# A decoder block on one core: the second weight folding is ordered later, zeroing and expert-weight loads go one piece a unit, and the whole order is planned anew

## The chip, the cores and the metric

The kernel runs on one core of one Trainium2 chip. The metric is the device time of the program in microseconds, lower is better. Durations of single steps come from one profiled execution.

## The reference

For x of 8 batches x 112 tokens x 256 the block adds three sub-layers, each on a normalised x:

```python
x = x + self_attention(layernorm(x))                      # 16 heads of 16, causal, with biases
x = x + cross_attention(layernorm(x), ctx, ctx, mask)     # ctx: 8 x 375 x 256, per-head 16x16 Wq, Wk, Wv
x = x + moe_gated_slot_attention(layernorm(x))            # below
```

Cross attention projects with small 16x16 matrices and ends in `out @ Wo.T + bo`. The third sub-layer (2 of 8 experts per token) is:

```python
x = rms_norm(h, norm_w); scores = softmax(x @ Wg.T); top 2 experts of each token
# tokens sorted by (batch, expert); per expert k, v, f = x @ W[e].T ; q = x @ Wq.T
# a gated recurrence over chunks of 64 tokens, scattered back and weighted:
out = (restored * rw).sum(2); return rms_norm(out, gnorm_w) @ Wo.T
```

## The kernel before

**Stages and units.** All work is cut into named stages, each on one engine: T (TensorE), V (VectorE), A (ScalarE), P (GpSimd), S (SyncE, which issues most DMAs). Attention runs in 48 units: `("s", b, h)` is half of a batch's self-attention heads, `("c", b, g)` a quarter of its cross-attention heads. A unit is a first score product `S`, a row maximum `max` on V, a transpose `mT`, a subtraction `q2` on V, the scores again transposed `st`, an exponential `exp` on A, the product with the values `pv`, and a copy `oT`. `UNITS` lists them: index 0 to 5 are the self-attention of batches 0 to 2, then three cross units, two self units of batch b + 3 and a fourth cross unit for each batch.

**The order.** A class `Plan` simulates the five engines with the costs of `COST`, the lags of `LAG`, the landing times of `LANDS`, a rank for each stage shifted by `BIAS`, an earliest time `at`, and a `SLACK` per engine by which stages that could start at nearly the same time are compared by rank. It writes one list of stages per engine, and each engine's program is that list, in order, with waits on semaphores. A change of any cost or bias can reorder all five lists and the choice of PSUM banks.

**Combining weights.** `combine 0` multiplies the cross Wq and Wk into `bdq`. `combine 1` multiplies Wv and Wo into `fo`: four matmuls on T behind `wait_ge(l_wo, 32)`, a semaphore of two DMAs (`wvo` and a row of `rw_sb`), and a copy `fo` on V (line 1235). Its product is first used by the output projection of cross attention of batch 0, `oproj 1 0`. In the plan it has `at=19.5`, and `oproj 0` (self attention) needs it too, though the program of `oproj 0` waits for nothing of it.

**The experts.** Tokens are routed in two groups (batches 0 to 4, 5 to 7). Their rows are scattered by GpSimd into a DRAM buffer `xs_d` that must hold zeros first: eight writes of 896 KB from SyncE (stage `zero`, line 753), each behind the first score product of a unit of `Z_UNITS`: units 3, 5, 7, 9, 11 for the first group, 30, 32, 34 for the second. Expert weights come by one load of 256 KB and eight of 768 KB (stage `later`, lines 758 and 760) behind units 12, 14, ..., 28 (`L_UNITS`). GpSimd then scales them with the norm weight (stage `fold`, two instructions for each expert, line 1709), in two halves that each wait for their four loads. Then 29 tiles of 128 gathered rows are multiplied with their expert's weights (`pkf`, `pvx`), whose offset in `wm` TensorE reads from a register; a stage `regs` loads all registers of a group (16, then 13) from SBUF at once. The tiles' results go to DRAM, are gathered by token and scanned (`scan`).

**The start.** SyncE's first DMA is x of batches 0 and 1 together; the norm of batch 0 waits for it.

Of the kernel before, what the change touches and what calls it, by code (L numbers as in the profile page):

```python
# [4 lines left out]
NB, S, D, NK = 8, 112, 256, 375  # L5
KC, NC3 = 125, 3
NE = 8
GROUPS = ((0, 1, 2, 3, 4), (5, 6, 7))
# [5 lines left out]
GNT = [(2 * c + NE * 127) // 128 for c in GCAP]  # L14
GT0 = [sum(GNT[:g]) for g in range(NG)]
GBASE = [NE * sum(GCAP[:g]) for g in range(NG)]
NT = sum(GNT)
ZROW = NE * S * NB
TG = [g for g in range(NG) for _ in range(GNT[g])]
# [18 lines left out]
            + ([("s", b + 3, 0), ("s", b + 3, 1)] if b + 3 < NB else []) + [("c", b, 3)]])  # L38
Z_UNITS = [UNITS[3 + 2 * i] for i in range(len(GROUPS[0]))] + [UNITS[30 + 2 * i] for i in range(NB - len(GROUPS[0]))]
L_UNITS = [UNITS[12 + 2 * i] for i in range(1 + NE)]  # L40

# [5 lines left out]
        "kTx": (0.19, 0.36), "kp": (1.77, 1.95), "logits": (0.9, 1.06), "mTc": (0.15, 0.31),  # L47
# [3 lines left out]
        "pvc": (0.62, 0.78), "pvs": (0.43, 0.59), "pvx": (0.86, 1.03), "qTx": (0.76, 0.92),  # L51
        "qgT": (0.19, 0.36), "qk": (1.79, 1.95), "regs": (0.5, 0.5), "siT": (0.19, 0.36),
        "stc": (1.43, 1.59), "sts": (0.98, 1.14), "stx": (0.89, 1.07), "tm": (0.48, 0.65),
# [35 lines left out]
BIAS = {  # L89
    "T": {"G": -67, "Sc": -161, "Ss": -925, "cb": 292, "fT": 212, "fo": 935, "inf": -17, "kTx": -152,  # L90
          "logits": -273, "onT0": -97, "oproj0": -37, "oproj1": 169, "pkf": 342, "pvs": 1037, "pvx": 181,
# [8 lines left out]
}  # L100
SLACK = {"T": 0.3, "V": 0.1, "A": 0, "P": 0.15, "S": 0}

# [23 lines left out]
class Plan:  # L126

    LAG = {"AP": 0.14, "AT": 0.145, "AV": 0.035, "PV": 0.04, "TA": 0.1, "TP": 0.27, "TV": 0.107, "VA": 0.035, "VP": 0.09,
           "VT": 0.146, "VV": 0.0, "PA": 0.1, "PT": 0.15}
    LANDS = {"later": 8.0, "zero": 8.0, "gx": 2.6, "gk": 2.8, "scatter": 3.0, "kd": 2.5, "ldmask": 4.0, "ldctx": 3.0, "ldctxT": 4.0}  # L130
    UNIT = ("S", "max", "mT", "q2", "st", "exp", "pv", "oT")
# [33 lines left out]
    def build(self):  # L165
# [9 lines left out]
        add("V", ("combine", 0), 0.6, -230, [("T", ("combine", 0))])  # L175
        add("T", ("combine", 1), 0.9, -230, release=("V", ("combine", 1)), at=19.5)
        add("V", ("combine", 1), 0.75, -230, [("T", ("combine", 1))])
# [3 lines left out]
        for b in range(NB):  # L181
# [7 lines left out]
            for h in range(2):  # L189
# [8 lines left out]
            add("P", ("pad", b), 0.83, 100 * b - 120, [("A", ("ones", RT)), ("T", ("pv", ("c", b - 2, 3)))] + ld("ldctx", 2),  # L198
                at=18.0 if b == 0 else 25.0)
            add("P", ("mkb", b), 1.55, 100 * b - 110, [("P", ("mkT", b - 1)), ("V", ("max", ("c", b - 2, 3), 3))]  # L200
                + ld("ldmask", 2), at=15.0 if b == 0 else 23.0)
            add("P", ("mkT", b), 1.37, 100 * b - 110, [("P", ("mkb", b)), ("T", ("st", ("c", b - 2, 3)))])
# [61 lines left out]
    def output(self, k, b, r):  # L264
        add = self.add
        last = [("A", ("oT", ("s", b, h))) for h in range(2)] if k == 0 else [("A", ("oT", ("c", b, g))) for g in range(4)]
        add("T", ("nrm", k, b), 0.42, r, last + [("T", ("onT", k, b - 1))], ("V", ("nrm", k, b)))
        add("V", ("nrm", k, b), 0.78, r, [("T", ("nrm", k, b))])
        add("T", ("onT", k, b), 0.2, r, [("V", ("nrm", k, b)), ("T", ("oproj", k, b - 1))], ("A", ("onT", k, b)))
        add("A", ("onT", k, b), 0.36, 0, [("T", ("onT", k, b))])  # L270
        add("T", ("oproj", k, b), 0.9, r, [("A", ("onT", k, b)), ("V", ("combine", 1))], ("V", ("oproj", k, b)), at=17.0)
        add("V", ("oproj", k, b), 0.43, r, [("T", ("oproj", k, b)), ("P", ("xn", k, b)), ("P", ("xn", 1, b - 2 if k == 0 else b))])
# [200 lines left out]
def decoder_kernel(nc, x, ctx, ctxT, mask, maskT, watt, bself, wx, wxvo, rows, wrouter, wmoe, wo_moe,  # L473
# [5 lines left out]
    with root:  # L479
# [216 lines left out]
        def _(e):  # L696
# [19 lines left out]

            e.dma_start(xbo[:, 0:2, :], x[:, 0:2, :]).then_inc(l_x0, 16)
            e.dma_start(cst[:, 0:128], consts[:, 0:128]).then_inc(l_id, 16)
            e.dma_start(wqk[:, 0, :, :], watt[:, 0, :, :]).then_inc(l_wq, 16)
            e.dma_start(bqk[:, :], bself[:, 0:8]).then_inc(l_bqk, 16)  # L720
            e.dma_start(wqk[:, 1, :, :], watt[:, 1, :, :]).then_inc(l_wk, 16)
            e.dma_start(cst[:, C_CB:C_CB + 224], consts[:, C_CB:C_CB + 224]).then_inc(l_cm, 16)
            e.dma_start(wv[:, :, :], watt[:, 2, :, :]).then_inc(l_wv, 16)
# [53 lines left out]
        def _(e):  # L777
# [8 lines left out]
            for stage in order["T"]:  # L786
# [162 lines left out]
                elif what == "regs":  # L949
                    e.wait_ge(v_tab, N_TAB_INC * (b + 1))  # L950
                    e.load(regs[GT0[b]:GT0[b] + GNT[b]], eti[0:1, GT0[b]:GT0[b] + GNT[b]])
                else:
# [6 lines left out]
                    elif what == "pkf":  # L959
# [3 lines left out]
                        for i in range(2):  # L963
                            off = e.snap(regs[t], min_val=0, max_val=(NE - 1) * WC)
                            last = mm(ps[:, bk, 0:512], xsT[:, r, 128 * i:128 * i + 128], wm[:, bass.ds(off + i * 768, 512)],
                                      i == 0, i == 1)
                        last.then_inc(t_pkf, 1)
                    elif what == "pvx":
                        for i in range(2):
# [113 lines left out]
        def _(e):  # L1083
# [88 lines left out]
            for stage in order["V"]:  # L1172
                what, b, bk = stage[0], stage[-1], slot.get(stage, [None])[0]
                k = stage[1] if len(stage) == 3 else None
                if what == "stats":
                    v = st[:, b, k, :]
                    src = x1[:, b % 2, :] if k == 1 else xbo[:, b, :]
                    if k == 0 and b in (0, 2, 4):
                        e.wait_ge((l_x0, l_x, l_late)[min(b // 2, 2)], (16, 16, 48)[min(b // 2, 2)])
                    elif k == 1:  # L1180
                        e.wait_ge(v_x1, b + 1)
                    elif k == 2:
                        e.wait_ge(v_x2, b + 1)
# [12 lines left out]
                elif what == "consts":  # L1196
                    e.wait_ge(l_id, 16)
                    e.tensor_copy(idb[:, :], ident).then_inc(v_cst, 1)
                    e.wait_ge(l_cm, 16)
                    e.tensor_copy(cmb[:, :, :], cst[0:S, C_CB:C_CB + S].unsqueeze(1).to_broadcast([S, 2, S])  # L1200
# [682 lines left out]
```

## Time and profile before

| | |
|---|---|
| median of 3 runs | 462.94 us (459.88 to 474.88) |
| profiled execution, its own time | 463.49 us |
| its span, first to last instruction | 461.7 us |
| TensorE busy in the span | 432.3 us (94%) |
| mean granted TensorE clock | 0.985 |
| VectorE, ScalarE, GpSimd busy | 66%, 53%, 39% |
| DMA | 51.07 MB, mean 111 GB/s |

The span is 1.8 us shorter than the profiled execution's own time. A clock of 1.00 is the upper of TensorE's two levels (2.4 GHz), 0.50 the lower (1.2 GHz); a value between is a stretch that had both. Busy times of PE are modelled at their ends, so a stall inside the array doesn't show as idle time.

### The profile page before, as it was taken

The numbers are of one execution on the slowest core, as the hardware profiler recorded it, in microseconds if no ns is written. First come the engines' busy times: TensorE is split into PE (matmuls) and PEld (weight loads), VectorE is DVE, ScalarE is ACT, GpSimd is POOL, SyncE is SP. The second block draws the span as 40 slices with busy tenths as digits, with TensorE's granted clock in tenths as the row PEclk, the third lists the DMA queues.
The fourth block names the chain that finished last, engine by engine and source line by source line (L and its number), as shares of the span: only waits on it lengthen the run. The fifth ranks groups of instructions, "written<-read, shape, count | busy, mean of one in ns | idle before, by whom it ended". The sixth has DMA issues, their size and how long they took to land.

```text
span 461.7 us, 12854 instructions
## 1 busy us (share of the span) xinstructions
PE 432.3 (94%) x4632; PEld 317.0 (69%) x4632; DVE 306.3 (66%) x1034; ACT 244.8 (53%) x663; POOL 179.7 (39%) x240
## 2 busy tenths in 40 slices
PE   8879899999999899997979999899899999999997
PEld 6656576867667577664646666565578766988885
DVE  4736757487577577676786559995366675876663
ACT  5123233425443434443536778787675876777652
POOL 5451033132732752145332268626543214444320
PEclk9989979999999899999999999999999999999999
DMA  7848323544436335011210244445723332121202
GB/s 205 170 128 289 122 81 115 158 139 111 135 136 156 123 106 155 3 35 41 55 38 25 92 143 134 152 161 176 227 62 103 105 110 104 65 75 53 66 11 61
DMA packets 23918, 51.07 MB, mean 111 GB/s; under 512 B 3105, under 2 KB 13546, under 8 KB 23858
## 3 DMA queue, kind: packets, MB, share of 16 engines
q1 hardware_dynamic: 20018, 38.02, 26.5%
q0 software_dynamic: 3440, 11.15, 8.9%
q10 hardware_dynamic: 400, 1.10, 0.8%
q8 instruction: 39, 0.64, 0.6%
q14 instruction: 21, 0.17, 0.1%
HBM read 28.75 MB, written 21.50 MB: 109 GB/s over the span
## 4 chain that ended last, share of the span: by engine, by line
PE 76%; DMA 7%; DVE 5%; ACT 3%; issue 3%; another core or an unknown queue 3%; SPq 2%; ACTq 1%; POOL 0%; DVEq 0%; POOLq 0%
PE ps L781 67%; PE ps L784 9%; DMA rw_sb<-in_rows 3%; DMA kv<-kd_d,idk 3%; DVE jnk L1259 1%; ACT pT L1529 1%; DMA kd_d<-kd 1%; ACT u L1586 0%; ACT u L1584 0%; SPq L714 0%; DVE kd L1390 0%; DVE kd L1384 0%; ACT u L1588 0%; ACTq L1498 0%
## 5 line engine op out<-in xcount | busy, mean ns | idle before, releaser
L1529 ACT ACTIVATE pT<-ps 125x672 f32<-125x672 f32 (+1 forms) x96 | 60.6, 666 | 93.0 <-PE ps L781 84.1
L781 PE MATMUL ps<-wm,xsT 128*128 x232 | 83.4, 492 | 0.5 <-ACT xsT L1579 0.5
L1259 DVE CUSTOM_DVE_ANT_0 jnk<-ps,mkb 112x375 bf16<-112x375 f32 x128 | 63.6, 544 | 21.7 <-PE ps L781 21.7
L781 PEld LDWEIGHTS ps<-wm,xsT 128*128 128x128 f32 x232 | 41.0, 190 | 24.3 <-issue 21.6
L1758 POOL DMA_INDIRECT xs<-xs_d,idg x29 | 28.9, 997 | 29.8 <-PE ps L784 22.1
L781 PE MATMUL ps<-cxT,cqT 32*112 32x375 f32 x256 | 28.7, 518 | 7.3 <-ACT pT L1529 3.1
L781 PE MATMUL ps<-q,cxT 32*125 32x112 f32 x768 | 30.7, 291 | 0.0
L781 PEld LDWEIGHTS ps<-q,cxT 32*125 32x125 f32 x768 | 24.9, 190 | 7.8 <-issue 7.6
L1803 POOL TENSOR_TENSOR qg<-okb,dc 112x256 f32<-112x256 f32 x16 | 11.8, 736 | 42.4 <-ACT okb L1627 42.3
L1264 DVE TENSOR_REDUCE mxz<-ps 112x2 f32<-112x224 f32 x64 | 21.0, 383 | 10.3 <-PE ps L781 10.3
L1384 DVE SCALAR_TENSOR_TENSOR kd<-ps,u 128x512 f32<-128x512 f32 x29 | 19.9, 685 | 9.0 <-ACT u L1588 7.4
L781 PE MATMUL ps<-pT,cxp 125*32 125x112 f32 x768 | 25.7, 267 | 0.0
L1627 ACT ACTIVATE okb<-okb,sm 112x64 f32<-112x64 f32 x64 | 21.4, 338 | 8.1 <-DVE sm L1436 8.1
L781 PE MATMUL ps<-mkT,idb 125*125 125x336 bf16 x128 | 24.6, 315 | 0.9 <-DVE xbo L1284 0.6
L1584 ACT ACTIVATE u<-ps 128x512 f32<-128x512 f32 x29 | 17.3, 596 | 14.4 <-PE ps L781 13.7
L1741 POOL DMA_INDIRECT xs_d<-y,idu x16 | 15.8, 990 | 21.2 <-DVE idu L1347 18.0
L1687 POOL TENSOR_SCALAR st<-st 112x1 f32<-112x1 f32 x16 | 3.8, 235 | 49.2 <-DVE st L1186 49.2
L781 PEld LDWEIGHTS ps<-pT,cxp 125*32 125x32 f32 x768 | 17.8, 111 | 7.3 <-ACT pT L1529 2.7
L781 PEld LDWEIGHTS ps<-mkT,idb 125*125 125x125 bf16 x128 | 16.0, 139 | 8.4 <-issue 3.1
L1796 POOL DMA_INDIRECT kv<-kd_d,idk x16 | 15.3, 955 | 15.8 <-issue 6.9
L1722 POOL TENSOR_SCALAR mkb<-mki 112x375 bf16<-112x375 int32 x8 | 12.2, 1524 | 20.2 <-DVE mxz L1259 14.1
L781 PEld LDWEIGHTS ps<-cxT,cqT 32*112 32x112 f32 x256 | 9.8, 173 | 14.9 <-ACT pT L1529 7.7
(242 smaller groups left out, 1059.2 us busy)
## 6 DMA issues: line engine op xcount, KB each, us to landing
kd_d<-kd SPq DMA_DIRECT2D x29, 384.0 KB
xs_d<-xs SPq DMA_DIRECT2D x8, 896.0 KB, 4.2
wm<-in_wmoe SPq DMA_DIRECT2D x8, 768.0 KB, 4.3
cxT<-in_ctxT SPq DMA_DIRECT2D x32, 93.8 KB, 3.4
cx<-in_ctx SPq DMA_DIRECT2D x8, 375.0 KB
mki<-in_mask SPq DMA_DIRECT2D x8, 164.1 KB
mti<-in_maskT SPq DMA_DIRECT2D x8, 164.1 KB
out<-xbo SPq DMA_DIRECT2D x8, 112.0 KB, 1.8
```

Source lines behind the costliest of these rows:

```text
L781: return e.matmul(o, l, r, start=start, stop=stop)
L784: return e.transpose(o, i, ident[0:n, 0:n])
L1259: e.tensor_tensor_reduce(jnk[:, j % 2, :], ps[0:S, bk, 0:NK], mkb[:, b % 2, :], 1.0, -3e38, ALU.add, ALU.max, mxz[:, n % 2, 0, c:c + 1]).t ...
L1264: e.tensor_reduce(mxz[:, n % 2, :, :].rearrange("p i m -> p (i m)")[:, c:c + 113:112], ps[0:S, bk, 0:2 * S].rearrange("p (g n) -> p g n", ...
L1384: e.scalar_tensor_tensor(kd[:, t % RD, 0:512], ps[:, slot["pkf", t][0], 0:512], 0.0, u[:, r, :], ALU.min, ALU.subtract).then_inc(v_ls, 1)
L1529: e.activation(pT[0:w, n % RP, 2 * i:2 * i + 2, 0:m], ps[0:w, b0:b1 + 1:b1 - b0, 0:m], ACT.Exp).then_inc(a_pT, 1)
L1584: e.activation(u[:, r, :], ps[:, slot["pkf", t][0], 0:512], ACT.Abs).then_inc(a_sp, 1)
L1627: last = e.activation(w, w, ACT.Exp, bias=s4[:, h:h + 1], accum_out=s4[:, 4 + h:5 + h])
L1722: e.tensor_scalar(mkb[:, b % 2, :], mki[:, b % 2, :], 0.0, -1e20, ALU.is_equal, ALU.mult).then_inc(p_mkb, 1)
L1741: e.indirect_dma_start(out=xs_d.ap(), out_offset=bass.IndirectOffsetOnAxis(ap=idu[:, k, b:b + 1], axis=0), in_=y[:, b % RY, :], in_offset= ...
L1758: e.indirect_dma_start(out=xs[:, t % RX, :], out_offset=None, in_=xs_d.ap(), in_offset=bass.IndirectOffsetOnAxis(ap=idg[:, t:t + 1], axis= ...
L1796: e.indirect_dma_start(out=kv[:, t % RK, :], out_offset=None, in_=kd_d[g].ap(), in_offset=bass.IndirectOffsetOnAxis(ap=idk[:, b, j:j + 1], ...
```

## The change

- `combine 1` goes from rank -230, `at=19.5` to rank -40, `at=42.0`, and only `oproj 1` needs it in the plan. Its instructions and waits are the same.
- The eight zero writes stand behind units 14 to 21, the nine loads of `wom` and the experts' weights behind units 24 to 32.
- `regs` loads two registers of a group; the register of tile t + 2 is loaded on TensorE after the first product of tile t.
- x of batch 0 is loaded alone as the first DMA, x of batch 1 five DMAs later with a semaphore shared with the causal masks (one more DMA on SyncE's queue).
- Earliest times of `pad` and `mkb` of the first batches, some costs, nearly all biases, the slacks of V, A and P, and the planned landing of `gk` change, so the order of all engines is planned anew.

```diff
-Z_UNITS = [UNITS[3 + 2 * i] for i in range(len(GROUPS[0]))] + [UNITS[30 + 2 * i] for i in range(NB - len(GROUPS[0]))]
-L_UNITS = [UNITS[12 + 2 * i] for i in range(1 + NE)]
+Z_UNITS = [UNITS[14 + i] for i in range(NB)]
+L_UNITS = [UNITS[24 + i] for i in range(1 + NE)]
...
-SLACK = {"T": 0.3, "V": 0.1, "A": 0, "P": 0.15, "S": 0}
+SLACK = {"T": 0.3, "V": 0.2, "A": 0.15, "P": 0.2, "S": 0}
...
-        add("T", ("combine", 1), 0.9, -230, release=("V", ("combine", 1)), at=19.5)
+        add("T", ("combine", 1), 0.9, -40, release=("V", ("combine", 1)), at=42.0)
...
-                at=18.0 if b == 0 else 25.0)
+                at=26.0 if b == 0 else 30.0)
...
-                + ld("ldmask", 2), at=15.0 if b == 0 else 23.0)
+                + ld("ldmask", 2), at=19.0 if b == 0 else 29.0)
...
-        add("T", ("oproj", k, b), 0.9, r, [("A", ("onT", k, b)), ("V", ("combine", 1))], ("V", ("oproj", k, b)), at=17.0)
+        add("T", ("oproj", k, b), 0.9, r, [("A", ("onT", k, b))] + ([("V", ("combine", 1))] if k else []), ("V", ("oproj", k, b)), at=17.0)
...
-            e.dma_start(xbo[:, 0:2, :], x[:, 0:2, :]).then_inc(l_x0, 16)
+            e.dma_start(xbo[:, 0:1, :], x[:, 0:1, :]).then_inc(l_x0, 16)
...
+            e.dma_start(xbo[:, 1:2, :], x[:, 1:2, :]).then_inc(l_cm, 16)
...
-                    e.load(regs[GT0[b]:GT0[b] + GNT[b]], eti[0:1, GT0[b]:GT0[b] + GNT[b]])
+                    e.load(regs[GT0[b]:GT0[b] + 2], eti[0:1, GT0[b]:GT0[b] + 2])
...
+                        if t + 2 < NT and TG[t + 2] == TG[t]:
+                            e.load(regs[t + 2:t + 3], eti[0:1, t + 2:t + 3])
```

## Rows read from the trace of the kernel before

**Rows 1.** The page: span and the engines' busy time.

```profile
span 461.7 us, 12854 instructions
...
PE 432.3 (94%) x4632; PEld 317.0 (69%) x4632; DVE 306.3 (66%) x1034; ACT 244.8 (53%) x663; POOL 179.7 (39%) x240
```

**Rows 2.** Windows: length, busy time of PE, PEld, DVE, ACT, POOL, clock, DMA.

```profile
22.60:25.30 2.70, 0.00 (x0) 0.00 (x0) 0.00 (x0) 0.18 (x1) 1.52 (x2) 1.00 0.64 173
...
167.00:197.00 30.00, 29.68 (x453) 22.26 (x452) 20.72 (x76) 13.14 (x31) 6.31 (x9) 1.00 0.34 100
...
206.00:240.00 34.00, 27.30 (x419) 18.48 (x421) 25.07 (x112) 13.90 (x33) 14.44 (x18) 1.00 0.16 43
```

**Rows 3.** Waits of PE: in total, times, longest, in us.

```profile
PE ps L781 <- DMA rw_sb<-in_rows: 3.3, 1, 3.3
```

**Rows 4.** Timeline about the second folding: start, duration, engine, instruction.

```profile
22.18 0.39 DVE L1243 TENSOR_TENSOR q<-qkT,ps 128x224 f32<-128x224 f32 x1 [0.99 <-PE ps L784]
...
25.36 1.10 PE L781 MATMUL ps<-wvo 128*128 128x256 f32 x4 [3.29 <-DMA rw_sb<-in_rows]
...
26.50 0.69 DVE L1235 COPY fo<-ps 128x512 f32<-128x512 f32 x1 [3.93 <-PE ps L781]
```

**Rows 5.** Windows of TensorE alone: busy time, granted clock, DMA share.

```profile
25.00:28.00 3.00, 2.64 (x32) 0.82 0.33 111
28.00:31.00 3.00, 3.00 (x28) 0.61 0.32 121
49.00:55.00 6.00, 5.18 (x63) 1.00 0.53 178
55.00:58.00 3.00, 1.44 (x21) 0.94 0.00 0
58.00:61.00 3.00, 2.93 (x26) 0.50 0.82 279
```

**Rows 6.** Timeline about the register loads of both groups.

```profile
233.64 0.90 PE L781 MATMUL ps<-cxT,cqT 32*112 32x375 f32 x8 [0.41 <-issue]
...
290.83 0.16 DVE L1137 TENSOR_SCALAR eti<-etr 1x13 int32<-1x13 f32 x1
...
292.32 0.99 PE L781 MATMUL ps<-W,yq 112*128 112x224 f32 x4 [1.53 <-issue]
293.15 2.75 PE L781 MATMUL ps<-wm,xsT 128*128 x8
```

**Rows 7.** SyncE's queue: zero writes, weight loads, a batch's context load.

```profile
41.06 28.07 SPq L753 DMA_DIRECT2D xs_d<-xs  x4
...
79.32 0.35 SPq L760 DMA_DIRECT2D wm<-in_wmoe  x1
83.24 1.72 SPq L714 DMA_DIRECT2D cxT<-in_ctxT  x4
...
92.98 15.01 SPq L760 DMA_DIRECT2D wm<-in_wmoe  x3
...
157.40 8.99 SPq L753 DMA_DIRECT2D xs_d<-xs  x2
```

**Rows 8.** Timeline: folds, a norm beside one, first scatter, first gather.

```profile
115.36 7.09 POOL L1709 TENSOR_SCALAR wm<-wm,nwc 128x768 f32<-128x768 f32 x8
...
147.14 1.20 POOL L1741 DMA_INDIRECT xs_d<-y,idu  x1 [3.56 <-DVE idu L1347]
...
164.68 1.83 POOL L1709 TENSOR_SCALAR wm<-wm,nwc 128x768 f32<-128x768 f32 x2
...
165.01 0.73 DVE L1193 TENSOR_SCALAR xn<-x,st 112x256 f32<-112x256 f32 x1
...
232.31 1.03 POOL L1758 DMA_INDIRECT xs<-xs_d,idg  x1 [3.13 <-DVE eti L1137]
```

**Rows 9.** The chain that ended last, two of its pieces.

```profile
206.39 3.58 another core or an unknown queue
...
211.71 3.46 another core or an unknown queue
```

More of the change, by code:

```diff
@@ L47 @@
         "kTx": (0.19, 0.36), "kp": (1.77, 1.95), "logits": (0.9, 1.06), "mTc": (0.15, 0.31),
[1 row of a table removed]
[1 row of a table added]
         "okx1": (1.19, 1.35), "onT0": (0.19, 0.35), "onT1": (0.2, 0.38), "oproj0": (0.87, 1.03),
[1 row of a table removed]
-        "pvc": (0.62, 0.78), "pvs": (0.43, 0.59), "pvx": (0.86, 1.03), "qTx": (0.76, 0.92),
-        "qgT": (0.19, 0.36), "qk": (1.79, 1.95), "regs": (0.5, 0.5), "siT": (0.19, 0.36),
-        "stc": (1.43, 1.59), "sts": (0.98, 1.14), "stx": (0.89, 1.07), "tm": (0.48, 0.65),
[2 rows of a table removed]
[1 row of a table added]
+        "pvc": (0.66, 0.79), "pvs": (0.43, 0.59), "pvx": (0.89, 1.03), "qTx": (0.76, 0.92),
+        "qgT": (0.19, 0.36), "qk": (1.79, 1.95), "regs": (0.6, 0.6), "siT": (0.19, 0.36),
+        "stc": (1.48, 1.62), "sts": (0.98, 1.14), "stx": (0.89, 1.07), "tm": (0.48, 0.65),
[2 rows of a table added]
         "am": (0.53, 0.62), "combine0": (0.34, 0.42), "combine1": (0.6, 0.69), "consts": (0.5, 0.58),
@@ L89 @@
 BIAS = {
-    "T": {"G": -67, "Sc": -161, "Ss": -925, "cb": 292, "fT": 212, "fo": 935, "inf": -17, "kTx": -152,
-          "logits": -273, "onT0": -97, "oproj0": -37, "oproj1": 169, "pkf": 342, "pvs": 1037, "pvx": 181,
[7 rows of a table removed]
+    "T": {"G": -5, "R": 118, "Sc": -228, "Ss": -774, "cb": 167, "fT": 291, "fo": 1376, "inf": 89, "kTx": -303,
+          "logits": 183, "nrm1": -300, "okx0": 127, "onT0": -150, "onT1": -365, "oproj0": -132, "oproj1": 60,
+          "ovx0": 93, "ovx1": -281, "pkf": 406, "pvs": 892, "pvx": 285, "qTx": 322, "siT": 302, "stx": -219,
+          "tm": -194, "v": 80, "x": -202, "xnT1": 105},
+    "V": {"kk": -858, "ls": -130, "maxc": -143, "maxs": -264, "msk0": 228, "nrm0": -169, "oo": -175,
+          "oproj0": -221, "pick": 79, "rwa": 254, "rwb": 45, "split": 298, "stats1": -296, "stats2": 427,
+          "tab0": 154, "tab14": 48, "tab3": 21, "tab5": 243, "tb4": 172, "xn0": 404},
+    "A": {"es": -328, "expc": 318, "exps": 337, "oTs": 226, "qgT": -609, "siT": 38, "x": 41, "xnT1": 222,
+          "yT": 311},
+    "P": {"gx": 166, "qTf": 147},
     "S": {},
 }
-SLACK = {"T": 0.3, "V": 0.1, "A": 0, "P": 0.15, "S": 0}
+SLACK = {"T": 0.3, "V": 0.2, "A": 0.15, "P": 0.2, "S": 0}
 def kind(stage):
@@ L129 @@
            "VT": 0.146, "VV": 0.0, "PA": 0.1, "PT": 0.15}
-    LANDS = {"later": 8.0, "zero": 8.0, "gx": 2.6, "gk": 2.8, "scatter": 3.0, "kd": 2.5, "ldmask": 4.0, "ldctx": 3.0, "ldctxT": 4.0}
+    LANDS = {"later": 8.0, "zero": 8.0, "gx": 2.6, "gk": 3.2, "scatter": 3.0, "kd": 2.5, "ldmask": 4.0, "ldctx": 3.0, "ldctxT": 4.0}
     UNIT = ("S", "max", "mT", "q2", "st", "exp", "pv", "oT")
@@ L1177, in _ @@
                     src = x1[:, b % 2, :] if k == 1 else xbo[:, b, :]
-                    if k == 0 and b in (0, 2, 4):
-                        e.wait_ge((l_x0, l_x, l_late)[min(b // 2, 2)], (16, 16, 48)[min(b // 2, 2)])
+                    if k == 0 and b in (0, 1, 2, 4):
+                        e.wait_ge((l_x0, l_cm, l_x, l_x, l_late)[min(b, 4)], (16, 32, 16, 16, 48)[min(b, 4)])
                     elif k == 1:
@@ L1198, in _ @@
                     e.tensor_copy(idb[:, :], ident).then_inc(v_cst, 1)
-                    e.wait_ge(l_cm, 16)
+                    e.wait_ge(l_cm, 32)
                     e.tensor_copy(cmb[:, :, :], cst[0:S, C_CB:C_CB + S].unsqueeze(1).to_broadcast([S, 2, S])
```

15 rows, old and new, of tables (BIAS, COST) are left out of this document.

## The prediction
> **What bounds the kernel now.** I read the page first: TensorE is busy 432.3 of 461.7 us, so it is idle for 29.4 us in all, while VectorE has 66% and GpSimd 39% [rows 1]. Such a kernel gets faster in three ways only: TensorE gets less work, its clock is lower for less time, or some of those 29.4 us close. Next I took TensorE's waits [rows 3]: the longest is 3.3 us, in one piece, for a DMA of `rw_sb`. The timeline shows where that first one sits: the four matmuls of the second folding start at 25.36 after 3.29 us of idle time, and VectorE's copy of the result had itself been idle 3.93 us [rows 4]. The window over the hole shows that nobody used it: in 22.60 to 25.30 PE, PEld and DVE have 0.00 us and ACT 0.18 us [rows 2]. Last I read stretches: 49 to 58 has 2.4 us idle [rows 5], 206 to 240 has 6.7, 167 to 197 only 0.3 [rows 2]. So the kernel is bound by TensorE's own work with a few holes, and the hole at 22 us is the one that the change names.
>
> **The change part by part.**
>
> *Second folding.* It keeps its four matmuls (1.10 us) and its copy (0.69 us) and moves them behind 42 us [rows 4]. The DMA that it waits for had landed when they started at 25.36, so behind 42 us it waits for nothing. In the list of TensorE the scores of unit 1 come next, and their input `q2` was written at 22.57 [rows 4]; they can start at once. All other engines were stopped by the same wait [rows 2], so everything behind moves up as a block: -3.3 us (bounds -2.7, the window without any PE or DVE work, and -3.3). What is late next is the first cross units at 49 to 58, where TensorE is busy 5.18 of 6 and then 1.44 of 3 us [rows 5]. If the four matmuls fall into that hole, another 1.1 us is gained; if they fall into the full stretch before it, nothing. The copy costs 0.69 us on VectorE near that place. I take 0, bounds -1.1 and +0.7.
>
> *Clock.* Behind the hole the granted clock was 0.82 for 3 us and 0.61 for 3 us [rows 5], a mixture of the 2.4 and the 1.2 GHz level. The work lost is 3 x 0.18 + 3 x 0.39 = 1.7 us. Without the hole the clock has no reason to fall there: -1.7 us, bounds -1.7 and 0. The Trainium skill says the same in TensorE: Matmul & The Clock Gate, "What's actually happening": the clock falls behind idleness and is released by activity. The trace agrees, since 55 to 58 with 1.44 us busy is also followed by 0.50 [rows 5]. That second dip I leave in, for the hole before it comes from the maxima on VectorE.
>
> *Registers.* Group 1's `regs` ends its input at 290.99 and the next matmul starts at 292.32, 1.53 us idle "issue": 13 loads in 1.33 us, 0.10 us each [rows 6]. Two loads cost 0.2, so -1.1. Group 0's 16 loads showed only 0.41 us of idle time [rows 6], since matmuls were still running: -0.3. Against this stand 25 single loads after the first products of tiles, 0.10 x 25 = 2.6 us if each were exposed. Eight matmuls of a tile run in 2.75 us without a gap, with register arithmetic between them [rows 6], so TensorE's sequencer is ahead there and I take 0. Together -1.4, bounds -1.4 and +1.2.
>
> *Start.* x of batch 0 alone is half the bytes. The first transposition needs the norm of batch 0 and the end of the warming matmuls at nearly one time; I take 0, bounds -0.4 and +0.5 (one more DMA issue ahead of the later loads).
>
> *Zeroing.* Four writes spread over 41 to 69 us (one earlier) go away from the start [rows 7]. TensorE had no other DMA wait worth a row, so that frees nothing by itself: 0. The new places follow from the same queue: a load behind unit 14 was issued at 79.32, those behind units 16, 18, 20 at 92.98 to 108, so the eight writes lie in 79 to about 117, and the loads behind units 24 to 32 end at 166 (the zero write behind unit 32 was the second of the two issued from 157.40) [rows 7]. The first scatter, which needs the first five zero writes, is issued at 147, and the first gather of rows for an expert's product at 232 [rows 8], long after either. Queued behind these waits on SyncE are masks, context and transposed context of the next batch. The load of `cxT` for batch 2 was issued at 83.24, four us behind a 768 KB load, for a product at 99; with 896 KB pieces in its place it lands in time. 0, bounds 0 and +2.
>
> *Folding on GpSimd.* Eight instructions took 7.09 us [rows 8], 0.89 each, sixteen 14.3 us. They move from 115 to 166 into about 150 to 197, behind the later loads. GpSimd is busy 6.31 of 30 us in 167 to 197 [rows 2], so there is room: 0, if the plan puts them there. What is queued behind them is the norm's variance and power, which VectorE's `xn` and TensorE's projection wait for; one stage of two instructions delays it by at most 1.8 us.
> A row also shows the two engines in each other's way: `xn` took 0.73 us while a fold ran [rows 8]. SBUF — State Buffer ("SBUF: two separate sides") of the Trainium skill says why this could be: GpSimd and VectorE share a port pair as an exclusive lock, and whoever comes second waits for the whole instruction. By that rule the fold costs VectorE up to 0.9 us each wherever VectorE works from SBUF, which would be the same count of folds in a stretch no less busy; since it moves the price and does not add one, my sum is the same by the rule and by the row.
>
> *Planned anew.* All lists may change, and no row shows the new one. The idle time that an order can touch is 29.4 less 3.3 already counted, and less about 6 at the two ends: 20 us. Bounds: -8 (nearly half of it closed) and +8 (as much again opened). I take 0: TensorE's work is the same, and 167 to 197 shows that an order can leave it 1% idle.
>
> **Sum.** -3.3 - 1.7 - 1.4 = -6.4 us. From the profiled execution's 463.49, which is 0.55 above the median of the runs, that is 457.1; I say 457.0. This is -1.3% from 462.94.
>
> **The rivals.**
>
> *The order gives the gain back (about 462).* The new order opens holes, for instance by a later `mkb` and `pad` at the first cross units, where 2.4 of 9 us are already idle [rows 5]. 5 us of new holes give 457 + 5 = 462. For it: such an order rests on hundreds of guessed costs. Against it: nothing in the diff adds a wait. It would also be this case if the folding stayed early or the sequencer could not hide the single register loads (+2.6, 459.6).
>
> *The order heals more (about 451).* 206 to 240 has 6.7 us of idle TensorE, and the chain has two pieces of 3.58 and 3.46 us there that no engine explains [rows 2, 9]; 49 to 58 has 2.4 [rows 5]. Closing two thirds of these 9.1 us gives 457 - 6 = 451. For it: the later folds and zeroes leave the first 70 us free, and the costs are nearer to the durations seen. Against: the unexplained pieces stand beside scatters, which stay as many.
>
> *The folds land on the chain (about 471, slower).* If the plan, which counts 8 us of landing for each load, puts the second half of the folds behind the scatters, they fall into 206 to 240, where GpSimd already has 14.4 of 34 us [rows 2] and everything waits for scatter, norm and gather in turn. All sixteen in a row are 14.3 us, and 457 + 14 = 471. It decides from the point where the last fold starts later than the first gather of rows (232 us before [rows 8]); up to 197 it costs nothing.
>
> **How the numbers follow.** The forecast has 0.50, the order that gives back 0.20, the one that heals 0.23, the folds 0.07. The range for 8 in 10 takes the forecast with its bounds and reaches most of both neighbours: 449 to 467. 2% is 9.3 us, about what a measurement of this kernel can tell from no change: faster means under 453.7, slower over 472.2. Most of the healing case and a little of the forecast's lower side are under 453.7: 0.25. Over 472.2 is part of the folds' case: 0.05. Within: 0.70.
>
> **What the profile of the changed kernel would show.** TensorE's wait for `rw_sb` gone, and no idle window near 22 us. `fo` copied after 42 us. The clock at 1.00 in 22 to 31. A gap of at most 0.5 us at each `regs`, and tiles' eight matmuls still near 2.75 us. Zero writes in 75 to 115, weight loads in 115 to 163, the last fold before 200. Idle time of TensorE near 25 us and a mean clock above 0.985. Wrong would be: a new hole longer than 2 us in TensorE's waits, a context load that TensorE waits for at a cross unit's start, folds past 230 us, or a second clock dip longer than before.

## The result and the profile after

The changed kernel takes 472.59 us (median of 6 runs, 471.22 to 473.63), the kernel before 462.88 on the same chip: a ratio of 1.021 (95% interval 1.018 to 1.024). It is slower by 9.7 us; the interval doesn't hold 1. The prediction was 457.0, with a range up to 467. Ratios, here and in all tables, leave out executions in a slower state that some of them fall into, while the times in the tables are medians of all, so a ratio isn't quite the quotient of two medians.

The page of the changed kernel, against [rows 1]. The last line is TensorE's granted clock in 40 slices, in tenths.

```profile
span 470.9 us, 12880 instructions
...
PE 435.1 (92%) x4632; PEld 315.7 (67%) x4632; DVE 313.9 (67%) x1034; ACT 245.4 (52%) x663; POOL 179.4 (38%) x240
...
PEclk8899999999999979999999999999999999999999
```

TensorE has the same 4632 matmuls, 2.8 us more busy time and 6.4 us more idle time. DVE has the same 1034 instructions and 7.6 us more busy time: VectorE's instructions have become longer, and that alone is a sign. The clock is low at the start and in slice 15 (165 to 177 us).

Its waits (total, times, longest), against [rows 3]:

```profile
PE ps L783 <- ACT sq L1568: 4.6, 1, 4.6
PE ps L783 <- ACT pT L1533: 4.0, 6, 1.0
PE ps L786 <- DVE xn L1197: 3.2, 1, 3.2
PE ps L786 <- DMA xs<-xs_d,idg: 2.5, 3, 1.4
```

The wait for `rw_sb` is gone. A wait of 4.6 us and one of 3.2 us are new, and so are waits for the gather of `xs`, 2.5 us in all.

Windows of before that were not shown, then those of after (length, busy time of PE, PEld, DVE, ACT, POOL, clock, DMA):

```profile
0.00:20.00 20.00, 16.96 (x133) 13.39 (x134) 12.68 (x40) 6.68 (x7) 11.20 (x30) 1.00 0.86 189
20.00:40.00 20.00, 15.60 (x202) 11.21 (x201) 8.21 (x23) 4.68 (x11) 6.14 (x7) 0.91 0.61 191
160.00:180.00 20.00, 19.82 (x261) 15.34 (x253) 14.71 (x51) 8.22 (x20) 8.96 (x14) 1.00 0.42 120
300.00:400.00 100.00, 96.56 (x600) 70.35 (x600) 65.28 (x190) 74.14 (x219) 39.34 (x47) 1.00 0.40 129
```

```profile
0.00:20.00 20.00, 14.54 (x76) 11.70 (x76) 8.49 (x28) 6.32 (x6) 9.78 (x29) 0.83 0.86 188
20.00:40.00 20.00, 18.77 (x269) 14.71 (x268) 11.64 (x36) 4.86 (x12) 7.59 (x9) 1.00 0.57 164
22.60:25.30 2.70, 2.70 (x36) 2.49 (x35) 2.17 (x7) 0.00 (x0) 1.49 (x2) 1.00 0.68 184
160.00:180.00 20.00, 14.40 (x181) 10.84 (x180) 13.27 (x31) 6.06 (x14) 11.13 (x12) 0.83 0.17 41
166.00:169.00 3.00, 0.45 (x3) 0.03 (x1) 3.00 (x1) 0.00 (x0) 3.00 (x4) 0.88 0.00 0
...
172.00:175.00 3.00, 3.00 (x32) 2.51 (x31) 0.69 (x2) 1.30 (x3) 0.00 (x0) 0.50 0.07 21
300.00:400.00 100.00, 92.32 (x540) 64.60 (x540) 61.53 (x165) 69.69 (x201) 40.48 (x48) 1.00 0.38 121
```

Busy time times clock is the work that TensorE did at full clock. From 0 to 20 us it fell from 16.96 to 14.54 x 0.83 = 12.1 (4.9 lost), from 20 to 40 it rose from 15.60 x 0.91 = 14.2 to 18.8 (4.6 gained, the hole of [rows 2] is full), from 160 to 180 it fell from 19.8 to 12.0 (7.9 lost), from 300 to 400 by 4.2. Together 12.4 are lost. In the same product by stretches of 20 us the changed kernel is only 3.9 behind at 460 us: 40 to 80 gives back 3.1, and 140 to 160 gives back 2.8, where the clock of before was 0.91. (The product is a guide and no exact account: summed over the whole span it is 4 us larger in the changed kernel.) The predicted gain is there and is cancelled at the start; two later places make the kernel slower, one at 162 us and one behind 300 us. The first is read now, the second with the third group of runs.

**The start.** Timelines of VectorE, then of TensorE:

```profile
7.34 0.43 DVE L1188 BATCH_NORM_STATS2 st<-xbo 112x6 f32<-112x256 f32 x1 [3.55 <-DMA cst<-in_consts]
7.80 0.18 DVE L1190 BATCH_NORM_AGGREGATE st<-st 112x2 f32<-112x6 f32 x1
7.90 0.38 DVE L1197 TENSOR_SCALAR xn<-xbo,st 112x256 f32<-112x256 f32 x1
```

```profile
8.43 0.61 PE L786 MATMUL ps<-cst,xn 112*128 112x112 f32 x2 [3.20 <-DVE xn L1197]
9.53 3.73 PE L783 MATMUL ps<-xnT,wqk 128*128 128x112 f32 x16 [0.49 <-ACT xnT L1516]
```

VectorE's list has the statistics of batch 1 ahead of `xn` of batch 0, as before. They now wait for `l_cm`, that is for x of batch 1 and for the causal masks behind it in the queue, and stand 3.55 us. `xn` of batch 0, whose x landed long before, stands behind them, TensorE waits 3.20 us for it, and after that hole its clock is low (the 16 matmuls take 3.73 us, where they took 2.01 before).

**At 162 us.** GpSimd, VectorE and TensorE:

```profile
162.25 7.07 POOL L1713 TENSOR_SCALAR wm<-wm,nwc 128x768 f32<-128x768 f32 x8
```

```profile
164.33 5.02 DVE L1311 TENSOR_TENSOR mk<-tk,k 112x16 f32<-112x16 f32 x1
169.27 0.54 DVE L1263 CUSTOM_DVE_ANT_0 jnk<-ps,mkb 112x375 bf16<-112x375 f32 x1
```

```profile
171.01 1.35 PE L783 MATMUL ps<-mkT,idb 125*125 125x336 bf16 x4 [4.57 <-ACT sq L1568]
```

`mk` compares 8 scores of a token with its two best: 16 elements a partition. It takes 5.02 us and ends at 169.35; the run of eight folds ends at 162.25 + 7.07 = 169.32. The maxima that TensorE's next unit needs stand behind it. TensorE has 0.45 us of work in 166 to 169, and when it works again its clock is 0.50 from 172 to 175. The profile puts the wait down to ScalarE's `sq`, which itself stood behind VectorE: a releaser's name isn't the cause.

The second half of the folds has moved too, in front of the scatters and the first gather (GpSimd). Before, the same scatter came at 207.28 us and the gather at 232.31 [rows 8]:

```profile
207.97 7.34 POOL L1713 TENSOR_SCALAR wm<-wm,nwc 128x768 f32<-128x768 f32 x8
...
215.49 1.05 POOL L1745 DMA_INDIRECT xs_d<-y,idu  x1 [0.18 <-issue]
...
239.59 1.03 POOL L1762 DMA_INDIRECT xs<-xs_d,idg  x1 [4.72 <-DVE eti L1141]
```

This run meets `mk` of another batch, and there it costs little (VectorE, and one of the folds):

```profile
209.69 0.17 DVE L1311 TENSOR_TENSOR mk<-tk,k 112x16 f32<-112x16 f32 x1
209.90 0.77 DVE L1329 TENSOR_TENSOR mb<-mk 112x16 bf16<-112x16 f32 x1
```

```profile
209.74 0.91 POOL L1713 TENSOR_SCALAR wm<-wm,nwc 128x768 f32<-128x768 f32 x1
```

`mk` comes 0.07 us before one fold ends and takes its usual 0.17 us. `mb` comes within the next, the fold shown, and takes 0.77 us where its median is 0.17: it ends at 210.67, that fold at 210.65, and five more folds follow. So one run held a VectorE instruction to the run's end, and the other only to the end of a fold.

### The profile page after: what moved, and what is told of

Same layout as the page of the kernel before. It is cut to its first block, busy times and chain, and to the rows that moved or that the text cites. A ratio compares the mean times of both kernels' runs of the same rounds, so it can differ in the third digit from the quotient of the medians.

```text
span 470.9 us, 12880 instructions
## 1 busy us (share of the span) xinstructions
PE 435.1 (92%) x4632; PEld 315.7 (67%) x4632; DVE 313.9 (67%) x1034; ACT 245.4 (52%) x663; POOL 179.4 (38%) x240
## 4 chain that ended last, share of the span: by engine, by line
PE 75%; ACT 7%; DVE 6%; issue 4%; DMA 4%; POOL 3%; SPq 1%; another core or an unknown queue 0%; ACTq 0%; DVEq 0%; POOLq 0%
PE ps L783 66%; PE ps L786 9%; DMA xs<-xs_d,idg 2%; ACT pT L1533 2%; POOL Wb L1777 1%; DVE jnk L1263 1%; DVE mk L1311 1%; DMA kv<-kd_d,idk 1%; ACT u L1590 1%; DMA cst<-in_consts 1%; ACT u L1588 1%; DVE qkT L1217 1%; ACT u L1592 1%; POOL W L1780 1%; POOL xs L1762 0%
## 5 line engine op out<-in xcount | busy, mean ns | idle before, releaser
L783 PE MATMUL ps<-xnT,wqk 128*128 128x112 f32 x128 | 17.8, 297 | 1.4 <-ACT xnT L1516 1.4
L1592 ACT ACTIVATE u<-u 128x512 f32<-128x512 f32 x29 | 18.3, 630 | 0.9
```

The lines of the kernel that those rows point to most:

```text
L783: return e.matmul(o, l, r, start=start, stop=stop)
L1592: e.activation(u[:, r, :], u[:, r, :], ACT.Ln, bias=1.0).then_inc(a_sp, 1)
```

## The experiments

The kernel before took 453.8, 467.9, 466.5 and 462.3 us in the four groups of runs, each on a chip of its own. So kernels are compared within their group, by their ratio to before or with one another. Where two groups are compared it is by ratios, and that is weaker: one kernel, b_wo, had 0.987 and 0.992 in two of them.

### First group: the start, and the folds beside `mk`

**a_x01**: the changed kernel with x of batches 0 and 1 in one transfer again (the waits on it go back too and aren't shown).

```
-e.dma_start(xbo[:, 0:1, :], x[:, 0:1, :]).then_inc(l_x0, 16)
+e.dma_start(xbo[:, 0:2, :], x[:, 0:2, :]).then_inc(l_x0, 16)
-e.dma_start(xbo[:, 1:2, :], x[:, 1:2, :]).then_inc(l_cm, 16)
```

> The changed kernel with x of batches 0 and 1 again in one first DMA; order of all engines unchanged. Theory 'two waits': VectorE's statistics of batch 1 stand in its list ahead of the normalisation of batch 0, and now wait for a transfer that lands at 7.3 us, so TensorE starts 2.7 us late and runs its first projections at the lower clock. Undone, TensorE's wait of 3.2 us for xn goes, the clock in 0 to 20 is 1.00 instead of 0.83, and the time is 4 to 6 us below the changed kernel's 472.6: 467 to 468.5. Rival 'the order': the start is made up later (the stall at 22 us of the kernel before was idle time too), and the loss sits in the new order of the expert and scan phases: within 1.5 us of 472.6.

**a_mk**: the changed kernel with `mk` as two instructions that have one SBUF tensor and a scalar of each partition.

```
-e.tensor_tensor(mk[:, :, b, :], tk[...].to_broadcast(...), k8[:, b, 0:2]..., ALU.is_equal)
+e.tensor_scalar(mk[:, 0, b, :], tk[:, b, 1, :], k8[:, b, 0:1], None, ALU.is_equal)
+e.tensor_scalar(mk[:, 1, b, :], tk[:, b, 1, :], k8[:, b, 1:2], None, ALU.is_equal)
```

> The changed kernel with VectorE's comparison that writes mk (both tensors in SBUF, one instruction) cut into two tensor_scalar instructions that read one tensor each; same values, same order. Theory 'two waits': the one instruction of 5.02 us at 164.3 was locked out by the run of eight folds on GpSimd and was not slow by itself; with one SBUF tensor it isn't held for the run, at most for one fold (0.9 us). TensorE's hole of 4.6 us at 166 to 171 and the low clock behind it (about 3 us of work) go: 465 to 468. Rival 'the order': the hole is made up by waits behind it: 471 to 473. Second rival, that the lock hits whatever VectorE instruction touches SBUF: one of the two new instructions takes some 5 us and the time stays at 472.

**a_foldtiny**: the folds scale 8 of the 768 columns; the rest of the expert weights stays unscaled.

```
-w = wm[:, b * WC + 768 * i:b * WC + 768 * i + 768]
+w = wm[:, b * WC + 768 * i:b * WC + 768 * i + 8]
```

> The changed kernel with each of the sixteen folds done on 8 of 768 columns, so that GpSimd is busy 14 us less; the other columns of the experts' weights are left unscaled. Theory 'two waits': as with mk alone, plus the 3 us by which the second run of folds (208.0 to 215.3) held the scatter of batches 2 and 3: 463 to 467. Rival 'the order': 471 to 473.

**a_foldnoread**: each fold writes a constant into the same 768 columns and reads nothing; the expert weights are lost.

```
-e.tensor_scalar(w, w, nwc[:, i:i + 1], 1.0, ALU.mult, ALU.mult).then_inc(p_fw, 1)
+e.memset(w, 0.5).then_inc(p_fw, 1)
```

> The changed kernel with each fold replaced by a memset of the same 768 columns (the experts' weights are then constants): GpSimd is busy about as long and writes SBUF, but reads none. If the lock is between GpSimd's reads and a VectorE instruction with two SBUF inputs, mk takes 0.2 us at 164 and the time is near that of the kernel with mk cut in two, 465 to 468. If any run of GpSimd work on SBUF holds VectorE, mk still takes 4 to 5 us and the time is 471 to 473.

| kernel | us | ratio to before (453.76) | 95% |
|---|---|---|---|
| a_x01 | 464.89 | 1.023 | 1.016 to 1.029 |
| a_mk | 470.29 | 1.036 | 1.030 to 1.042 |
| a_foldtiny | 462.24 | 1.018 | 1.012 to 1.025 |
| a_foldnoread | 461.13 | 1.016 | 1.010 to 1.021 |

a_mk kept both losses, so it is the base in this group, in which the changed kernel itself wasn't run. That has a cost: a_mk's ratio, 1.036, is above the changed kernel's 1.021 and 1.023 on other chips, so a part of every difference to a_mk may be the price of a_mk's own edit, and a_x01's ratio, 1.023, is no better than the changed kernel's. VectorE in a_mk (its run of folds: 162.61 to 169.68):

```profile
164.13 5.58 DVE L1311 TENSOR_SCALAR mk<-tk,k 112x8 f32<-112x8 f32 x1
169.62 0.22 DVE L1312 TENSOR_SCALAR mk<-tk,k 112x8 f32<-112x8 f32 x1
```

The first of the two is held to the end of the run at 169.7, the second, an equal instruction, takes 0.22 us. So it isn't only the form with two tensors that is held, and this repair fails. a_foldtiny, then GpSimd and VectorE of a_foldnoread:

```profile
164.43 0.17 DVE L1311 TENSOR_TENSOR mk<-tk,k 112x16 f32<-112x16 f32 x1
```

```profile
161.94 5.50 POOL L1713 MEMSET wm<- 128x768 f32 x8
```

```profile
163.47 0.17 DVE L1311 TENSOR_TENSOR mk<-tk,k 112x16 f32<-112x16 f32 x1
```

Short folds (eight in 1.97 us from 162.93): `mk` takes 0.17 us beside them, TensorE is busy 19.64 of the 20 us from 160 to 180 at full clock, and the kernel is 8.1 us faster than a_mk. Eight writes of the full size, from 161.94 to 167.44 and so right over `mk`, don't hold it either, and the kernel is 9.2 us faster. What holds `mk` in the form with two tensors is GpSimd reading SBUF, not GpSimd being busy or writing there. Writes aren't free for all, though. The second run of writes, from 200.32 to 205.81, meets a conversion with one SBUF tensor (`idu`, median 0.17 us):

```profile
203.86 1.98 DVE L1351 CAST idu<-idf 112x4 int32<-112x4 f32 x1
```

It ends at 205.84, with that run. The Trainium skill, SBUF — State Buffer, "SBUF: two separate sides", says that VectorE's instruction with two SBUF inputs competes with a GpSimd instruction that reads SBUF, one in a 2-port mode with any GpSimd instruction, and that the later one waits for one whole instruction. The traces agree on the two inputs (memset: not held). That the form with one tensor was held, and `idu` by writes, fits the other half, but which mode they ran in no trace shows. The traces disagree on the length: `mk` waited for the rest of one fold and five to seven more.

a_x01 removes the wait at the start (clock 1.00 and 16.85 us busy from 0 to 20) and is 5.4 us below a_mk, with the reservation above. In it `mk` is still held, for 5.60 us.

### Second group: parts of the change put into the kernel before

**b_wo**: before, with the two DMAs of the second folding issued earlier, right behind the load of `wxs`; the plan is untouched.

```
 e.dma_start(wxs[:, :], wx).then_inc(l_wx, 16)
+e.dma_start(wvo[:, :], wxvo).then_inc(l_wo, 16)
+e.dma_start(rw_sb[:, 2:3, :]..., rows[512:768]...).then_inc(l_wo, 16)
...
 load_ctx(0)
-e.dma_start(wvo[:, :], wxvo).then_inc(l_wo, 16)
-e.dma_start(rw_sb[:, 2:3, :]..., rows[512:768]...).then_inc(l_wo, 16)
```

> The kernel before, with the two DMAs that the second folding of weights waits for issued right behind wxs instead of behind the first context; order of all engines unchanged. It takes away the stall of 3.3 us at 22 us and nothing else. Theory of the prediction: everything behind moves up as a block, and the clock in 25 to 31 stays at 1.00: 462.9 - 3.3 - 1.7 = 458, at most 459.5. Rival: the next transfer (masks, transposed context, now later) stalls in its place, or the gain is lost in the chains at 200 to 240: 461.5 to 463.5.

**b_regs**: before, with the register loads of the change alone (two at first, then one behind each tile's first product).

> The kernel before with the register loads of the change alone (two at the group's start, then one in each tile). Theory of the prediction: the gap of 1.53 us before 292 shrinks to 0.4, group 0 gains at most 0.3, the loads inside tiles are hidden: 461.5. Rival: each of the 25 loads is exposed at 0.10 us: 464. Second rival: the gap sits beside a wait of another engine and the time stays at 462.9.

**b_split**: before, with x of batch 1 split off as in the change.

> The kernel before with x of batch 1 loaded apart, five DMAs later, as in the change; order of all engines unchanged. VectorE's list has the statistics of batch 1 ahead of the normalisation of batch 0 here too. Theory 'two waits': TensorE's first transposition comes at 8.4 instead of 5.75 us, clock 0.83 in 0 to 20, and the stall at 22 us for rw_sb, which is set by a DMA and not by TensorE, shrinks by as much: 1 to 3 us slower than 462.9, 464 to 466. Rival 'absorbed': the stall at 22 takes it all: 462.5 to 463.5.

**a_x01_mk**: the changed kernel with the edits of a_x01 and a_mk together.

> The changed kernel with both repairs, x of batches 0 and 1 in one DMA and mk in two instructions. Theory 'two waits': their gains add, 472.6 - 5 - 6 = 461.5 (460 to 463.5), so the rest of the change (order, unit places, late folding, registers) is worth about 1 us or nothing against 462.9. Rival 'the order': above 467.

| kernel | us | ratio to before (467.93) | 95% |
|---|---|---|---|
| b_wo | 462.52 | 0.987 | 0.977 to 0.996 |
| b_regs | 469.27 | 1.003 | 0.998 to 1.007 |
| b_split | 466.80 | 0.994 | 0.988 to 1.000 |
| a_x01_mk | 476.72 | 1.011 | 1.001 to 1.021 |

b_wo: without the wait TensorE is busy 19.59 us of 20 to 40 at full clock, where before had 15.60 at 0.91. This is the gain that was forecast, measured alone (by moving the two DMAs, not the folding). b_regs: TensorE's idle time put down to "issue" falls from 2.1 us to

```profile
PE ps L781 <- issue: 0.8, 2, 0.4
```

and the time doesn't follow. In the changed kernel itself such a gap is still there: `eti` of group 1 is written at 293.33 and the next matmul starts at 294.61, 1.28 us later and 1.16 of them idle, with two registers to load instead of 13; before it was 1.33 us. So that gap isn't 0.10 us for each load. b_split has the loss of the start in full (0 to 20: 14.70 us busy at 0.83) and yet isn't slower: from 20 to 40 it is busy 18.94 us. TensorE comes to the four matmuls that needed `rw_sb` at 27.22 us, behind the 25.36 at which they started before, so that wait is gone and has taken up the delay. (The trace is of an execution of 473.2 us, above the median.) So a loss at the start costs nothing that the time shows as long as the hole at 22 us is there. a_x01_mk is held for 4.97 us all the same, as a_mk showed.

### Third group: both repairs, and the units

**c_after**: the changed kernel again. 

> The changed kernel unchanged, so that the three beside it have their base on the same chip. Its ratio to the kernel before was 1.021 (1.018 to 1.024). The runs with one repair have been on chips where the kernel before took 454 and 468 us, and their ratios (1.023, 1.018, 1.016) don't add up to a repair worth 5 or 8 us unless the change costs more than 2% on such a chip. Theory one: the ratio is a property of the kernels and is 1.02 here too. Rival: it depends on the chip, and comes out between 1.01 and 1.035.

**c_x01_spread**: x joined, and the fold stages taken apart in GpSimd's list.

```
+for i, where in enumerate([("pad", 5), ("mkT", 5), ("mkb", 6), ("xn", 1, 6),
+                           ("scatter", 2), ("stats", 2, 4), ("pad", 7), ("scatter", 3)]):
+    order["P"].remove(("fold", i))
+    order["P"].insert(order["P"].index(where) + 1, ("fold", i))
```

> Both repairs in one, with the whole computation kept: x1 back in x0's transfer, and the eight fold stages taken apart in GpSimd's order, one behind each of pad 5, mkT 5, mkb 6, xn (1, 6), scatter 2, stats (2, 4), pad 7 and scatter 3. Theory (the two places are where the time went): no clock fall in 0 to 20, no VectorE instruction held for over 1.8 us (one fold stage), PE's idle in 160 to 180 under 1 us, 9 to 13 us less than the changed kernel, ratio to the kernel before 0.99 to 1.00. Rival (the new order as a whole costs, the two places are only what one sees first): the holes are gone and the ratio to before is still 1.005 or more, with TensorE's idle time after 300 us as in the changed kernel.

**c_x01_units**: x joined, and `Z_UNITS` and `L_UNITS` as in the kernel before, all planned with the new costs.

> The changed kernel with x1 back in x0's transfer and the old units for the zeroing and the expert weights (every second unit from 3, 30 and 12), planned with the new costs; the planner then puts the folds as two runs of eight instructions at the old places, ahead of mkb 4 and ahead of scatter 0. Theory (the later transfers moved the fold runs onto VectorE's mask and index work): no hold of mk, less than the changed kernel by 9 us or more, and as fast as the spread folds within 3 us. Rival (the units don't matter, the rest of the new order does): over 1.005 of before, and the same idle time after 300 us.

**b_wo_split**: before, with the edits of b_wo and b_split.

> The kernel before with the second folding's weights taken out of the queue that it waits for, and x1's transfer split off as in the change. The first alone gave 0.987 (0.977 to 0.996), the second alone 0.994 (0.988 to 1.000), where the wait at 22 us took up what the start lost. Theory (the start's loss is real and was only hidden there): with the stall gone the split costs 3 to 5 us, so 0.993 to 1.000. Rival (a loss at the start is taken up by other waits later): 0.987 as without the split.

| kernel | us | ratio to before (466.51) | 95% |
|---|---|---|---|
| c_after | 475.25 | 1.023 | 1.015 to 1.031 |
| c_x01_spread | 466.08 | 1.000 | 0.996 to 1.004 |
| c_x01_units | 467.22 | 1.002 | 0.999 to 1.006 |
| b_wo_split | 465.35 | 1.000 | 0.996 to 1.005 |

c_after has the ratio of the first comparison again, 1.023 against 1.021. c_x01_spread is 9.2 us faster than it. Both places are mended: 17.00 us busy at full clock from 0 to 20, 19.73 from 160 to 180. One hold is left, over both folds of a stage and from 0.37 us before them, while GpSimd issues an indirect DMA (VectorE, then GpSimd):

```profile
215.72 2.20 DVE L1314 TENSOR_TENSOR mk<-tk,k 112x16 f32<-112x16 f32 x1
```

```profile
216.09 1.80 POOL L1716 TENSOR_SCALAR wm<-wm,nwc 128x768 f32<-128x768 f32 x2
```

The two places had cost 5.4 and 8.1 to 9.2 us against a_mk in the first group, and here they bring 9.2 together. Some of the rest is missing in the scan:

```profile
320.00:340.00 20.00, 17.06 (x88) 12.86 (x89) 8.04 (x18) 11.84 (x42) 4.17 (x6) 0.74 0.32 98
```

TensorE is busy 17.06 us at 0.74: 12.6 us of work where before had 17.1.

c_x01_units is the telling miss. The folds are near the old places again, and one run meets `mk` of the new order, earlier than before (VectorE, GpSimd, windows):

```profile
149.76 6.47 DVE L1310 TENSOR_TENSOR mk<-tk,k 112x16 f32<-112x16 f32 x1
```

```profile
149.12 7.09 POOL L1712 TENSOR_SCALAR wm<-wm,nwc 128x768 f32<-128x768 f32 x8
```

```profile
140.00:160.00 20.00, 13.57 (x185) 9.60 (x186) 15.81 (x42) 5.20 (x12) 10.91 (x14) 0.81 0.35 115
160.00:180.00 20.00, 17.64 (x213) 12.57 (x215) 11.24 (x40) 7.57 (x19) 6.29 (x6) 0.85 0.34 102
```

149.76 + 6.47 = 156.23, the run of folds ends at 156.21. So the hold doesn't need the later transfers; any plan that knows nothing of it can put a run beside `mk`. But the transfers' units cost as well. c_x01_units has the hold and is as fast as c_x01_spread, which doesn't have it there. And it differs from a_x01 in the two lists of units alone, both with `mk` held (6.47 and 5.60 us), and has a ratio of 1.002 (0.999 to 1.006) against 1.023 (1.016 to 1.029), though in another group. The traces show where, behind 300 us (a_x01, c_x01_spread, c_x01_units):

```profile
300.00:400.00 100.00, 94.39 (x570) 67.57 (x568) 58.98 (x153) 69.59 (x212) 39.28 (x47) 0.98 0.38 119
```

```profile
300.00:400.00 100.00, 93.12 (x552) 66.98 (x551) 55.45 (x139) 67.38 (x205) 36.83 (x44) 0.95 0.36 112
```

```profile
300.00:400.00 100.00, 99.23 (x618) 71.87 (x616) 66.58 (x182) 77.91 (x229) 44.71 (x53) 1.00 0.40 131
```

With the later units TensorE waits there for the gather of `xs` (1.4 us in a_x01 and in the changed kernel) and for `xsT` (1.4); in c_x01_units it waits for neither. The DMAs of the units are long over at 300 us (the last is issued at 180.56 in the changed kernel), so it is the order planned from them that differs.

In the kernel before the runs at 115.36 and 156.76 met VectorE instructions that had an input from PSUM, which weren't held:

```profile
115.37 0.42 DVE L1274 TENSOR_TENSOR on<-ps,sm 112x256 f32<-112x256 f32 x1
```

b_wo_split: with the hole at 22 us gone the same split that was free in b_split costs what the edit of b_wo gains alone (1.3% in the second group, 0.8% in the fourth; this one is a comparison between groups, and its interval just touches that of the fourth).

### Fourth group: the hold taken away under the old units

**d_units_spread**: c_x01_units, and the last four fold stages taken apart.

```
+for i, where in ((4, ("scatter", 1)), (5, ("pad", 5)), (6, ("mkb", 6)), (7, ("xn", 1, 6))):
+    order["P"].remove(("fold", i))
+    order["P"].insert(order["P"].index(where) + 1, ("fold", i))
```

> The changed kernel with x1 in x0's transfer, the old units for zeroing and expert weights, and in GpSimd's order the last four fold stages taken apart (one each behind scatter 1, pad 5, mkb 6 and xn (1, 6)). The kernel with the same units and the folds as a run of eight had mk held for 6.5 us, and TensorE was 8.8 us short of full in 140 to 180 with the granted clock at 0.81 and 0.85. Theory (the holds are all that was wrong with the change): mk takes 0.17 us, the clock stays at 1.00 in 140 to 180, 8 to 11 us less than with the run of eight, ratio to before 0.975 to 0.985. Rival (the new order as a whole costs about 1%): the hold goes, and the ratio stays at 0.99 or more.

**d_wo**: b_wo again.

> The kernel before with only the second folding's weights taken out of the queue that it waits for, again. It was 0.9865 (0.977 to 0.996). Theory: the same here, 0.985 to 0.99, and so no faster than the changed kernel with old units, x1 joined and folds taken apart. Rival: it is the faster of the two by over 0.5%, and the new order is worth nothing.

| kernel | us | ratio to before (462.33) | 95% |
|---|---|---|---|
| d_units_spread | 454.78 | 0.989 | 0.984 to 0.995 |
| d_wo | 458.39 | 0.992 | 0.989 to 0.996 |

The windows of d_units_spread:

```profile
140.00:160.00 20.00, 19.51 (x265) 13.76 (x265) 14.87 (x63) 8.81 (x22) 5.32 (x6) 1.00 0.36 115
160.00:180.00 20.00, 17.99 (x299) 12.84 (x301) 10.61 (x38) 8.83 (x20) 10.12 (x11) 1.00 0.50 160
300.00:400.00 100.00, 99.19 (x681) 75.11 (x681) 67.35 (x181) 75.12 (x235) 44.30 (x53) 1.00 0.37 119
```

`mk` takes 0.18 us (at 148.43), the clock stays at 1.00, and the ratio falls from 1.002 to 0.989, 1.3% or 6 us, for four stages moved in one engine's list. This is again a comparison between groups; the two intervals don't overlap. From 300 to 400 TensorE is busy 99.19 us, more than before's 96.56. Against c_x01_spread, with the later units, the ratio is 1.1% lower (0.989 against 1.000, intervals apart), which is what the units cost, together with the one hold left there. The result lies between the two expectations, just above the theory's 0.985 and with an interval that holds both edges. It is the fastest kernel of the study; its interval overlaps that of d_wo, so that it beats the small edit d_wo isn't shown.

## Why the prediction was wrong

**"Second folding" and "Clock": held.** -3.3 and -1.7 were forecast. The window of [rows 2] is full, and b_wo and d_wo, which remove that wait alone, took 1.3% and 0.8% off by their ratios (6.3 and 3.5 us; forecast 5.0).

**"Start": failed.** The step took 0, with +0.5 at most, because it looked at the arrival of x of batch 0 and at TensorE's first transposition, and counted one more DMA issue. What it left out is the second half of the edit: the statistics of batch 1 got a wait, on x of batch 1 and the causal masks, and stand ahead of `xn` of batch 0 on VectorE. It measured 3.2 us of waiting and a clock of 0.83 from 0 to 20: 4.9 us of work in the windows, 5.4 us between a_mk and a_x01 (at most, see there), and it took b_wo's gain away in b_wo_split. The question that would have found it, what is queued behind a waiting instruction, was asked of SyncE and not of VectorE. b_split adds that the loss was invisible before only because a later hole took it up: two edits, one free and one better by itself, were not independent.

**"Folding on GpSimd": failed, and it is the largest term.** The step counted the folds (sixteen before and after) and said that a lock on the port "moves the price and does not add one". The price depends on what the folds meet. In the kernel before they met instructions that read PSUM, and one `xn` that took 0.73 for 0.41 us [rows 8]; I took that row as the size of such a meeting. The last fold was forecast before 200 us and began at 214.41. `mk`, an instruction of 0.17 us, is held 5.0 us, TensorE runs dry and its clock falls: 7.9 us of work lost from 160 to 180. a_foldtiny and a_foldnoread show it by 8.1 and 9.2 us against a_mk, d_units_spread by 6 us against the same kernel with the run in one piece. Both the rule (one whole instruction, so up to 0.9 us each) and my row were too small for this meeting, by the rest of the run; for those of the second run, 0.77 us for `mb`, they were right.

**"Registers": the gap closed in b_regs, the time stayed.** -1.4 was forecast; b_regs lost 1.3 us of "issue" idle and measured 1.003 (0.998 to 1.007). A gain of 1.4 us would be 0.997 and lies just outside. In the changed kernel the gap at group 1 was 1.16 us and not at most 0.5, so the term's price for a load, 0.10 us, is not shown.

**"Zeroing": no wait for it, the places later than forecast.** TensorE waits for none of the later zero writes or context loads. The last zero write is issued at 139.90 and the last weight load at 180.56, where the step had about 117 and 166; that is how the folds came later. Its two bounds were not tried alone.

**"Planned anew": inside its bounds of 8, and not 0.** Of the changed kernel's loss 4.2 us lie in 300 to 400. a_x01 and c_x01_spread have the later units and that loss, c_x01_units and d_units_spread have the old units and a full stage there, with the same costs and biases. So it comes with the unit lists, through the order that is planned from them, and is worth about 1% (c_x01_spread against d_units_spread). The step took units and order as two terms of 0 each. Which stages of the new order open the gaps stays open: the lists were changed only together, and no single stage was moved there.

**The rivals.** "The folds land on the chain" named the right engine with the wrong mechanism. Its point of decision, a last fold later than the first gather, was not reached: the last fold began at 214.41, the gather at 239.59. The second run did stand in front of a scatter, and that delay wasn't measured by itself. The case was given 0.07, and slower 0.05, because a fold seemed to cost only GpSimd's own queue.

## What to carry to other kernels

When a transfer is split, follow the wait of its second half: everything behind that instruction in its engine's list now waits too, and a loss at one place may be free only while a later hole takes it up. When transfers move to other places in a planned order, compare the stages far behind them too. A run of GpSimd instructions that work on SBUF can be one long lock for a VectorE instruction that works from SBUF alone: look for what such a run meets, keep it in short pieces, and put the pieces beside VectorE work from PSUM. Look for VectorE instructions that are far above the median of their group before you trust the releaser that a wait names.

## What the runs showed of the hardware

VectorE's `mk` normally takes 0.17 us (0.23 in the form with one tensor). It took 5.02, 5.60, 5.58, 4.97, 4.95 and 6.47 us in six traces beside a run of eight GpSimd `tensor_scalar` instructions of 0.9 us, and ended each time within 0.04 us of the end of the run. There the waiting instruction didn't get in between two instructions of the run. The form with one tensor of 8 elements and a scalar was held as the form with two tensors.

Elsewhere it did get in. In the second run of the changed kernel `mb` (two inputs from SBUF) took 0.77 us and `idu` (one) 0.46 us for 0.17, each to the end of a fold with more folds behind it; a_mk, a_x01, a_x01_mk and c_after show the same. `xn` (112x256, from SBUF) met two folds in the kernel before and came through in 0.73 us [rows 8], 0.15 us behind the end of the first. What decides between the end of one instruction and the end of the run stays open.

Sixteen `memset` instructions of the same size held no VectorE instruction with two SBUF inputs (`mk` 0.17 us in both runs of a_foldnoread), but held the conversion `idu` for 1.98 us, to the end of their run. VectorE instructions with an input from PSUM kept their 0.42 us beside a run of folds.
